# L0 cross-attention: keys normalised by features on GpSimd in four waiting steps, VectorE's norms in small pieces

## The chip, the cores and the metric

One Trainium2 chip, one core. The metric is the device time of one launch of a whole 12-layer kernel in microseconds; the kernel before took 3076.74 us (median of three runs, 3074.42 to 3076.98). The change touches one of the layers, L0's cross-attention (`l0_xattn`), which lies at the start.

## The reference

The input x is 8 x 64 x 256 and the context `ctx_1024` is 8 x 1601 x 256, all float32. The layer takes the normalised x as latents and attends over the context and the latents themselves:

```python
xn = layernorm(x, ln_x_g, ln_x_b)            # the context, 1601 tokens a batch
ln = layernorm(latents, ln_l_g, ln_l_b)      # 64 tokens a batch
q = (ln @ Wq) ...                            # 16 heads of 64
kv = concatenate([xn @ Wkv, ln @ Wkv])       # 1665 keys
qn = rmsnorm(q, qn_g) * scale;  kn = rmsnorm(k, kn_g)
sim = where(mask, einsum('bhid,bhjd->bhij', qn, kn), max_neg)
out = einsum('bhij,bhjd->bhid', softmax(sim), v) @ Wout + bout
```

Here layernorm is over the 256 features of a token (eps 1e-5) and rmsnorm over the 64 of a head.

## The kernel before, in words

The layer runs 64 steps: for each of 8 batches (b) eight steps (p), each of which does one pair of heads. Five instruction streams are written out by hand, one for an engine, and wait for each other by semaphores; the order inside a stream is the order of the code.

The context of a batch is held in two forms. `keys_tok` (the code's `xn`) has tokens on the partitions, 13 tiles of 128 tokens, and is used by the mix (probabilities times tokens; the values' projection comes after the mix, on 64 rows). `keys_feat` (`xnT`) has features on the partitions, 2 x 1665 columns, and is used by the projection of keys. Both have two buffers, one for the batch under work and one for the next.

The batch after is prepared inside the steps of the batch before: SP loads its tokens behind step 1; VectorE takes statistics (`ctx_stats`, bn_stats and bn_aggr, 7 and 6 tiles, at the end of steps 1 and 2), ScalarE makes the reciprocal root by Ln and Exp (`ctx_rstd`), VectorE normalises in place (`ctx_norm`, 7 tiles at the end of step 2 and 6 at the end of step 3, each L1385), GpSimd applies gain and bias (`gains`, L1558 and L1560) and then builds the mask row (`mask_row`, L1569). In steps 5 and 6 TensorE transposes the finished tokens of the next batch into features (`turn_keys`, L1727, 26 transposes a batch, in groups of 4, 3, 4 and 2 for each half of the features), and ScalarE and VectorE copy them out of PSUM (`keys_turned`, L1616 and L1441).

One step s on TensorE, in order: projection of the keys of step s+1, first half (L1742); transposes of the probabilities of step s-1, groups 0 and 1 (L1783); second half of the projection; groups 2 and 3; the transposes of the mixed sums of s-2 (L1814); the first part of the mix of s-1 (L1805); means of squares for s+1 (L1749); more mix; the scores of s (L1766); values of s-2 (L1823); more mix, an exchange of maxima between halves (L1791), the rest of the mix.

The same step on VectorE: copy of the keys' first half out of PSUM (L1446, 833 columns); copy of transposed probabilities (L1479, L1480); copy of the second half (L1446); L1479 and L1480 again; the product of keys and their scale, in two halves (`keys_normed`, L1456, both inputs in SBUF); the clamp of the mean squares of s+1 (`key_clamp`, L1450); the masked scores with their maximum, one for each head of the pair (`score_max`, L1466); the copy of a result (L1497); the negated maximum, the "shift" (L1471); and the division of the mix of s-1 (`divide`: L1487, L1489, L1492).

ScalarE squares the keys, copies transposed probabilities (L1644), makes the reciprocal norms of the keys of s+1 (L1625, L1627), stores them to DRAM (L1632, the scale rows) and then takes the exponentials of s (L1638), which wait for the shift. SP broadcasts the scale rows from DRAM to 2 x 64 partitions (`spread_scale`, L1340), and its loads for the next batch follow behind those in its queue. The scores' waits (`scores`, L1766) are for the product of s and the clamp of s+1.

## Time and profile before

| what | value |
|---|---|
| median of three runs | 3076.74 us (3074.42 to 3076.98) |
| the profiled execution's own time | 3077.33 us |
| its span | 3075.0 us |
| TensorE busy (PE) | 2774.9 us, 90% |
| VectorE busy (DVE) | 1690.4 us, 55% |
| ScalarE busy (ACT) | 1118.8 us, 36% |
| GpSimd busy (POOL) | 517.1 us, 17% |
| mix matmuls of this layer, L1805 | 431.2 us in 1664 |
| key projections of this layer, L1742 | 383.0 us in 1024 |
| mean granted clock of TensorE | 0.953 of full speed |

PE stands for TensorE, PEld for its weight loads, DVE for VectorE, ACT for ScalarE and POOL for GpSimd; SPq, ACTq and the like are an engine's queue at the issue of a DMA. A row of the timeline gives the start in microseconds from the start of the span, the length (of all instructions merged into the row, from the first's start to the last's end), engine, line of the kernel, operation, what is written <- what is read, shapes and count, and in brackets how long the engine stood idle before it and what released it. The first 16 of 40 slices of the span (77 us each) are this layer, and TensorE's busy share there is nearly always nine tenths.

### The profile page before, as it was taken

How to read it: one execution, taken by the hardware profiler on the slowest of the kernel's cores; microseconds unless marked ns; L12 is line 12 of the kernel's file. 1: busy time of each engine (PE TensorE's matmuls, PEld its weight loads, DVE VectorE, ACT ScalarE, POOL GpSimd, SP SyncE). 2: the span in 40 equal slices, each digit the busy share in tenths (PEclk: the TensorE clock that was granted, in tenths of full speed). 3: DMA queues.
4: the chain of work that ended last, by engine and by line, in shares of the span. 5: the costliest groups of instructions: out<-in, count | busy, mean ns of one | idle time of the engine just before them, and what ended most of it. 6: DMA issues, size and time to landing. Idle time of an engine off the chain costs nothing. (4 is left out here: it accounts for less than half of the span.)

```text
span 3075.0 us, 43440 instructions
## 1 busy us (share of the span) xinstructions
PE 2774.9 (90%) x17334; PEld 1876.2 (61%) x17334; DVE 1690.4 (55%) x3756; ACT 1118.8 (36%) x1993; POOL 517.1 (17%) x288
## 2 busy tenths in 40 slices
PE   5899999999999999789999977999996788979978
PEld 2566656566666666455565544665794456958846
DVE  5557575756566554545555545775452151057755
ACT  2343333333333332214555445662231161311123
POOL 2012020202020100000000000773001041045502
PEclk9899999999999999889999989999998997989989
DMA  4222232131322221131000000113686726743201
GB/s 149 49 54 71 52 77 71 46 82 46 77 51 72 46 57 35 58 133 44 23 33 33 1 6 15 46 42 107 239 309 193 227 56 245 276 161 141 70 13 35
DMA packets 93074, 272.45 MB, mean 89 GB/s; under 512 B 7874, under 2 KB 58074, under 8 KB 86218
## 3 DMA queue, kind: packets, MB, share of 16 engines
q1 hardware_dynamic: 88874, 260.70, 27.1%
q0 software_dynamic: 2976, 8.13, 0.7%
q8 instruction: 138, 2.26, 0.3%
q10 hardware_dynamic: 1024, 0.86, 0.1%
q14 instruction: 62, 0.51, 0.1%
HBM read 257.69 MB, written 11.45 MB: 88 GB/s over the span
## 5 line engine op out<-in xcount | busy, mean ns | idle before, releaser
L1805 PE MATMUL L_xattn_bank<-L_xattn_keys_tok,L_xattn_probsT 128*128 128x257 f32 x1664 | 431.2, 398 | 9.0 <-ACT L_xattn_probsT L1644 0.4
L1742 PE MATMUL L_xattn_wide<-L_xattn_keys_feat,weights_a 128*128 128x512 f32 (+2 forms) x1024 | 383.0, 517 | 1.3 <-DVE L_xattn_k_rnorm L1450 0.7
L1805 PEld LDWEIGHTS L_xattn_bank<-L_xattn_keys_tok,L_xattn_probsT 128*128 128x128 f32 x1664 | 300.3, 192 | 95.4 <-issue 34.4
L1742 PEld LDWEIGHTS L_xattn_wide<-L_xattn_keys_feat,weights_a 128*128 128x128 f32 x1024 | 190.8, 191 | 152.0 <-issue 125.3
L1446 DVE COPY L_xattn_k_normed<-L_xattn_wide 128x833 f32<-128x833 f32 (+1 forms) x128 | 131.0, 1024 | 183.2 <-PE L_xattn_wide L1742 183.2
L2751 DVE TENSOR_TENSOR_SCAN L_attn_state<-L_attn_decay,L_attn_banks 128x1024 f32<-128x1024 f32 x80 | 182.7, 2286 | 69.3 <-PE L_attn_banks L2953 61.3
L2021 DVE CUSTOM_DVE_ANT_0 L_xattn_scores<-L_xattn_banks,L_xattn_mask 128x512 f32<-128x512 f32 (+1 forms) x256 | 131.5, 570 | 151.8 <-issue 151.8
L1638 ACT ACTIVATE L_xattn_scores<-L_xattn_scores,L_xattn_neg_max 128x897 f32<-128x897 f32 x128 | 126.5, 1036 | 211.0 <-DVE L_xattn_neg_max L1471 211.0
L1558 POOL TENSOR_TENSOR L_xattn_keys_tok<-L_xattn_keys_tok,weights_a 128x1792 f32<-128x1792 f32 (+2 forms) x24 | 56.5, 2354 | 860.9 <-DVE L_xattn_keys_tok L1385 860.9
L2857 POOL TENSOR_TENSOR L_attn_state<-L_attn_state,L_attn_C_rows 128x1024 f32<-128x1024 f32 x80 | 188.7, 2360 | 70.0 <-DVE L_attn_state L2751 69.9
L1466 DVE CUSTOM_DVE_ANT_0 L_xattn_scores<-L_xattn_wide,L_xattn_mask_row 128x897 f32<-128x897 f32 x128 | 134.9, 1088 | 115.7 <-issue 115.7
L2953 PEld LDWEIGHTS L_attn_banks<-L_attn_B_diagonal,L_attn_dt_u_tok 128*128 128x128 f32 x1280 | 150.1, 193 | 66.3 <-issue 64.7
L2087 ACT ACTIVATE L_xattn_probsT<-L_xattn_banks 128x512 f32<-128x512 f32 (+1 forms) x208 | 122.7, 597 | 163.4 <-PE L_xattn_banks L2159 163.4
L3546 PE MATMUL L_ffn_banks<-L_ffn_slot_features,L_ffn_expert_w 128*128 128x128 f32 x1440 | 168.2, 277 | 3.0 <-DVE x_tok L3376 3.0
L2953 PE MATMUL L_attn_banks<-L_attn_B_diagonal,L_attn_dt_u_tok 128*128 128x128 f32 x1280 | 164.9, 283 | 3.9 <-ACT L_attn_B_diagonal L2813 3.9
L3546 PEld LDWEIGHTS L_ffn_banks<-L_ffn_slot_features,L_ffn_expert_w 128*128 128x128 f32 x1440 | 165.4, 194 | 3.9 <-DVE x_tok L3376 3.8
L1644 ACT ACTIVATE L_xattn_probsT<-L_xattn_bank 128x512 f32<-128x512 f32 x128 | 76.3, 596 | 230.4 <-PE L_xattn_bank L1783 230.4
L2159 PE MATMUL L_xattn_banks<-const,L_xattn_scores 128*128 128x128 f32 (+1 forms) x832 | 134.1, 288 | 24.7 <-DVE L_xattn_V L2012 10.7
L1783 PE MATMUL L_xattn_bank<-const,L_xattn_scores 128*128 128x128 f32 x896 | 120.8, 274 | 21.7 <-DVE L_xattn_probsT L1480 19.9
L1621 ACT ACTIVATE L_xattn_k_square<-L_xattn_k_normed 128x833 f32<-128x833 f32 (+1 forms) x128 | 115.2, 900 | 64.2 <-DVE L_xattn_k_normed L1446 61.1
L2159 PEld LDWEIGHTS L_xattn_banks<-const,L_xattn_scores 128*128 128x128 f32 (+1 forms) x832 | 88.8, 142 | 79.3 <-issue 45.8
L2844 POOL TENSOR_TENSOR L_attn_D_diagonal<-const,weights_a 128x256 f32<-128x256 f32 x2 | 1.2, 614 | 805.8 <-POOLq L909 805.8
(509 smaller groups left out, 4734.6 us busy)
## 6 DMA issues: line engine op xcount, KB each, us to landing
L_xattn_k_scale<-L_xattn_k_scale_rows SPq DMA_DIRECT2D x128, 417.0 KB, 5.0
L_xattn_ctx_feat<-in_ctx_feat SPq DMA_DIRECT2D x24, 1601.0 KB, 10.9
L_ffn_expert_w<-in_x_L_ffn SPq DMA_DIRECT2D x16, 2056.0 KB, 8.3
L_ffn_expert_w<-in_x_L_ffn SPq DMA_DIRECT2D x17, 1024.0 KB, 5.4
L_ffn_expert_w<-in_x_L_ffn SPq DMA_DIRECT2D x15, 1028.0 KB, 5.5
L_xattn_keys_tok<-in_ctx_tok SPq DMA_DIRECT2D x8, 1536.0 KB
L_attn_C_rows<-L_attn_c_rows SPq DMA_DIRECT2D x48, 256.0 KB, 3.2
L_xattn_ctx_tok<-in_ctx_tok SPq DMA_DIRECT2D x8, 1536.0 KB
```

The costliest lines, as they stand in the source:

```text
L1446: nc.vector.tensor_copy(kn[:, s % 2, a:a + n], ps).then_inc(k_copied, 1)
L1466: nc.vector.tensor_tensor_reduce(sc2[:, h, 0:SCORES], ps, mrow[b % 2][:, 1 - h:1 - h + SCORES], 1.0, -3.0e38, ALU.add, ALU.max, mx[:, h:h ...
L1638: nc.scalar.activation(sc2[:, h, 0:SCORES], sc2[:, h, 0:SCORES], ACT.Exp, bias=nm[:, h:h + 1]).then_inc(exp_ready, 1)
L1742: last = nc.tensor.matmul(wide[:, 2 * h + c, 0:n], wk[:, k, p * P:(p + 1) * P], xnT[b % 2][:, k, a:a + n], start=(k == 0), stop=(k == KT - 1))
L1805: last = nc.tensor.matmul(bS[:, 0:D + 1], pT[:, c, a, :, :].rearrange("p h q -> p (h q)"), xn[b % 2][:, t, :], start=(i == 0), stop=(i == ...
L2021: nc.vector.tensor_tensor_reduce(sc[:, j, a:a + n], ps[:, j, 0:n], mk[:, a:a + n], 1.0, -3.0e38, ALU.add, ALU.max, mx[:, j, c:c + 1]).then ...
L2087: nc.scalar.activation(pT[0:r, i % RING, :, :], ps[0:r, 6 + n % 2, :].rearrange("p (a n) -> p a n", n=P), ACT.Copy).then_inc(pT_ready, 1)
L2159: last = nc.tensor.transpose(ps[0:r, 6 + n % 2, j * P:(j + 1) * P], sc[:, j, t * P:t * P + r], L.ident)
L2751: nc.vector.tensor_tensor_scan(h[:, p % RING, :, :].rearrange("p m n -> p (m n)"), dA[:, p % RING, :, :].rearrange("p m n -> p (m n)"), ba ...
L2857: nc.gpsimd.tensor_tensor(state, state, C[:, g % C_RING, :].unsqueeze(1) .broadcast_to([P, 2, N]), ALU.mult).then_inc(hC_ready, 1)
L2953: last = nc.tensor.matmul(banks[:, i + j, t * P:(t + 1) * P], duT[d][:, t, m * P:(m + 1) * P], diag[:, g % DIAG_RING, t, :], start=True, s ...
L3546: last = nc.tensor.matmul(bank[:, c, :], w1[:, k, f:f + P], xT[:, j % 2, k, :], start=(k == 0), stop=(k == KT - 1))
```

## The change

For all batches but the first, `keys_feat` is no longer made by transposes. SP loads the context a second time, laid out by features (`load_feat`, behind step 2). VectorE's statistics and norms are cut into pieces of one to four tiles and stand at four places of a step (`between`: in front of the first copy of keys, in front of the second, behind the clamp, in front of the division). After the reciprocal roots, TensorE transposes the 26 columns of means and roots once (`turn_norms`, step 3's last group of transposes, which runs in the fifth step), VectorE copies the 26 x 128 result out, SP stores it to DRAM and broadcasts it to all partitions as two rows of 1601 columns (`spread_norms`, queued behind the scale rows of step 4). GpSimd then subtracts the mean and multiplies by the root over 128 x 1602, twice each (`keys_by_feature`), and ScalarE applies gain and bias, a column each, in one activation for each half of the features (`keys_gained`, step 6), and copies the 64 own keys (`own_keys`). The gains of the token form move to steps 6 and 7. In front of its subtractions, multiplications and the two gains GpSimd waits for VectorE's product of steps 4, 5, 6 and 7 (`keys_scaled`). The first batch is prepared as before. The weights grow by two columns each for gain and bias. (`-` and `+` lines of the diff follow, cut to its core: new semaphores and buffers, memsets of unused columns and unchanged names are left out.)

```diff
+                def load_feat(b):
+                    if b >= 2:
+                        sp.wait_ge(k_projected, 2 * NQ * (b - 1))
+                    feat = L.aps["ctx_feat"][b].rearrange("(k p) n -> p k n", p=P)
+                    sp.dma_start(xnT[b % 2][:, :, 0:FIRST], feat[:, :, 0:FIRST]).then_inc(feat_loaded[b % 2], 16)
+                    sp.dma_start(xnT[b % 2][:, :, SCORES:CTX + 1], feat[:, :, FIRST:CTX]).then_inc(feat_loaded[b % 2], 16)
+                def spread_norms(b):
+                    sp.wait_ge(norm_cols_ready, b)
+                    for i in range(2):
+                        sp.dma_start(norm_rows[b % 2, i].rearrange("(t n) -> t n", n=P), norm_cols[i:2 * TILES:2, :]
+                                     ).then_inc(norm_stored, 16)
+                    sp.wait_ge(norm_stored, 32 * b)
+                    if b >= 2:
+                        sp.wait_ge(feat_scaled, 2 * (b - 1))
+                    for i in range(2):
+                        sp.dma_start(norm_bc[:, i, 0:FIRST], norm_rows[b % 2, i:i + 1, 0:FIRST].broadcast_to([P, FIRST])
+                                     ).then_inc(norm_moved, 16)
+                        sp.dma_start(norm_bc[:, i, SCORES:CTX + 1],
+                                     norm_rows[b % 2, i:i + 1, FIRST:CTX].broadcast_to([P, CTX - FIRST])
+                                     ).then_inc(norm_moved, 16)
...
+                    if p == 2 and b < B - 1:
+                        load_feat(b + 1)
+                    if p == 4 and b < B - 1:
+                        spread_norms(b + 1)
...
                 def weights_turned(s, g):
                     h, a, n = GROUPS[g]
+                    b, p = divmod(s, NQ)
+                    if g == 3 and p == 3 and b + 1 < B:
+                        norms_turned(b + 1)
...
+                def norms_turned(b):
+                    dve.wait_ge(norm_turned, b)
+                    if b >= 2:
+                        dve.wait_ge(norm_stored, 32 * (b - 1))
+                    nc.vector.tensor_copy(norm_cols[:, :], bT[0:2 * TILES, 1, 384:384 + P]).then_inc(norm_cols_ready, 1)
+                stats_at = {(1, 2): range(0, 3), (1, 3): range(3, 7), (2, 0): range(7, 10), (2, 1): range(10, TILES)}
+                norm_at = {(2, 2): (range(0, 4),), (2, 3): (range(4, 6),), (3, 0): (range(6, 7), range(7, 9)),
+                           (3, 1): (range(9, 11),), (3, 2): (range(11, TILES),)}
+                def between(s, place):
+                    b, p = divmod(s, NQ)
+                    if b + 1 < B:
+                        if (p, place) in stats_at:
+                            ctx_stats(b + 1, stats_at[p, place])
+                        for tiles in norm_at.get((p, place), ()):
+                            ctx_norm(b + 1, tiles)
...
+                    between(s, 0)
                     if ahead:
                         key_copy(s + 1, 0)
                     if behind:
                         weights_turned(s - 1, 1)
+                    between(s, 1)
                     if ahead:
                         key_copy(s + 1, 1)
...
                     if ahead:
                         key_clamp(s + 1)
-                    if turns:
-                        keys_turned(b + 1, p - 5, 0)
+                    between(s, 2)
                     if s < STEPS:
                         score_max(s)
...
-                    if turns:
-                        keys_turned(b + 1, p - 5, 1)
-                    if s < STEPS and b + 1 < B:
-                        if p == 1:
-                            ctx_stats(b + 1, 0)
-                        if p == 2:
-                            ctx_stats(b + 1, 1)
-                            ctx_norm(b + 1, 0)
-                        if p == 3:
-                            ctx_norm(b + 1, 1)
+                    between(s, 3)
                     if behind:
                         divide(s - 1)
...
+                def keys_scaled(b, step):
+                    pool.wait_ge(kn_ready, 2 * (NQ * (b - 1) + step) + 2)
+
+                def keys_by_feature(b):
+                    pool.wait_ge(feat_loaded[b % 2], 32 * ((b + 1) // 2))
+                    pool.wait_ge(norm_moved, 64 * b)
+                    keys_scaled(b, 4)
+                    for k in range(KT):
+                        x = xnT[b % 2][:, k, 0:CTX + 1]
+                        nc.gpsimd.tensor_tensor(x, x, norm_bc[:, 0, :], ALU.subtract).then_inc(feat_shifted, 1)
+                    keys_scaled(b, 5)
+                    for k in range(KT):
+                        x = xnT[b % 2][:, k, 0:CTX + 1]
+                        pool.wait_ge(feat_shifted, 2 * (b - 1) + k + 1)
+                        nc.gpsimd.tensor_tensor(x, x, norm_bc[:, 1, :], ALU.mult).then_inc(feat_scaled, 1)
                 for b in range(B):
+                    if b:
+                        keys_by_feature(b)
+                        keys_scaled(b, 6)
                     gains(b, 0)
+                    if b:
+                        keys_scaled(b, 7)
                     gains(b, 1)
                     mask_row(b)
...
+                def keys_gained(b, k):
+                    act.wait_ge(feat_scaled, 2 * (b - 1) + k + 1)
+                    x = xnT[b % 2][:, k, 0:CTX + 1]
+                    g, o = at["ln_x_gc"] + k, at["ln_x_bc"] + k
+                    nc.scalar.activation(x, x, ACT.Identity, scale=w[:, g:g + 1], bias=w[:, o:o + 1]
+                                         ).then_inc(feat_ready, 1)
+                def own_keys(b):
+                    own = L.zT[:, :, b * S:(b + 1) * S]
+                    act.wait_ge(feat_ready, 3 * b - 1)
+                    nc.scalar.activation(xnT[b % 2][:, :, CTX + 1:KC], own[:, :, 0:S - 1], ACT.Copy)
+                    nc.scalar.activation(xnT[b % 2][:, :, FIRST:SCORES], own[:, :, S - 1:S], ACT.Copy).then_inc(feat_ready, 1)
...
-                    if b + 1 < B and p in (2, 3):
-                        ctx_rstd(b + 1, p - 2)
-                    if turns:
-                        keys_turned(b + 1, p - 5, 0)
-                        keys_turned(b + 1, p - 5, 1)
+                    if b + 1 < B and p == 2:
+                        ctx_rstd(b + 1, 1)
+                    if b + 1 < B and p == 6:
+                        for k in range(KT):
+                            keys_gained(b + 1, k)
+                        own_keys(b + 1)
                     if s < STEPS:
                         exponentials(s)
...
-                    if g < 2 and p in (5, 6) and b + 1 < B:
-                        pe.wait_ge((xT_act, xT_dve)[g], 4 * (b + 1) + 2 * (p - 5) + 2)
...
+                    if g == 3 and p == 3 and b + 1 < B:
+                        turn_norms(b + 1)
+
+                def turn_norms(b):
+                    pe.wait_ge(ctx_rstd_ready, 4 * b + 4)
+                    nc.tensor.transpose(bT[0:2 * TILES, 1, 384:384 + P], mv[:, :, :].rearrange("p t i -> p (t i)"),
+                                        L.ident).then_inc(norm_turned, 1)
...
-                    if turns:
-                        turn_keys(b + 1, p - 5, 0)
-                        turn_keys(b + 1, p - 5, 1)
```

## Rows read from the trace of the kernel before

**Rows 1.** The timeline of VectorE, the shift (L1471) of seven of the 64 steps.

```profile
97.77 0.16 DVE L1471 SCALAR_TENSOR_TENSOR L_xattn_neg_max<-L_xattn_max,L_xattn_bank 128x2 f32<-128x2 f32 x1 [0.48 <-PE L_xattn_bank L1791]
...
543.26 0.16 DVE L1471 SCALAR_TENSOR_TENSOR L_xattn_neg_max<-L_xattn_max,L_xattn_bank 128x2 f32<-128x2 f32 x1 [0.58 <-PE L_xattn_bank L1791]
...
560.15 0.16 DVE L1471 SCALAR_TENSOR_TENSOR L_xattn_neg_max<-L_xattn_max,L_xattn_bank 128x2 f32<-128x2 f32 x1 [0.57 <-PE L_xattn_bank L1791]
...
581.73 0.16 DVE L1471 SCALAR_TENSOR_TENSOR L_xattn_neg_max<-L_xattn_max,L_xattn_bank 128x2 f32<-128x2 f32 x1 [0.58 <-PE L_xattn_bank L1791]
...
598.86 0.16 DVE L1471 SCALAR_TENSOR_TENSOR L_xattn_neg_max<-L_xattn_max,L_xattn_bank 128x2 f32<-128x2 f32 x1 [0.60 <-PE L_xattn_bank L1791]
...
617.08 0.16 DVE L1471 SCALAR_TENSOR_TENSOR L_xattn_neg_max<-L_xattn_max,L_xattn_bank 128x2 f32<-128x2 f32 x1 [1.19 <-PE L_xattn_bank L1791]
...
1096.17 0.16 DVE L1471 SCALAR_TENSOR_TENSOR L_xattn_neg_max<-L_xattn_max,L_xattn_bank 128x2 f32<-128x2 f32 x1 [0.54 <-PE L_xattn_bank L1791]
```

**Rows 2.** The timeline of TensorE in the slow third step.

```profile
570.73 0.55 PE L1783 MATMUL L_xattn_bank<-const,L_xattn_scores 128*128 128x128 f32 x3 [2.85 <-DVE L_xattn_probsT L1480]
```

**Rows 3.** Stretches of time: busy us and count per engine, clock, DMA share, GB/s.

```profile
561.00:578.00 17.00, 14.02 (x61) 7.63 (x63) 14.06 (x31) 5.58 (x9) 7.43 (x2) 0.90 0.14 31
```

**Rows 4.** The timeline of VectorE from the second to the fourth step.

```profile
543.33 2.38 DVE L1370 BATCH_NORM_STATS2 L_xattn_ctx_stats<-L_xattn_keys_tok 128x6 f32<-128x256 f32 x7
...
562.93 2.35 DVE L1385 TENSOR_SCALAR L_xattn_keys_tok<-L_xattn_keys_tok,L_xattn_ctx_mean_var,L_xattn_ctx_rstd 128x256 f32<-128x256 f32 x7
...
565.90 3.32 DVE L1492 TENSOR_SCALAR L_xattn_mixed_tokens<-L_xattn_mixed_sum,L_xattn_rsum 128x256 f32<-128x256 f32 x1
...
584.45 2.23 DVE L1492 TENSOR_SCALAR L_xattn_mixed_tokens<-L_xattn_mixed_sum,L_xattn_rsum 128x256 f32<-128x256 f32 x1
...
590.87 2.69 DVE L1456 TENSOR_TENSOR L_xattn_k_normed<-L_xattn_k_scale,L_xattn_k_normed 128x834 f32<-128x834 f32 x2
...
596.01 1.09 DVE L1466 CUSTOM_DVE_ANT_0 L_xattn_scores<-L_xattn_wide,L_xattn_mask_row 128x897 f32<-128x897 f32 x1 [1.94 <-issue]
```

**Rows 5.** The timeline of GpSimd.

```profile
55.13 2.63 POOL L1558 TENSOR_TENSOR L_xattn_keys_tok<-L_xattn_keys_tok,weights_a 128x1280 f32<-128x1280 f32 x1 [1.52 <-DVE L_xattn_keys_tok L1385]
...
565.36 3.71 POOL L1558 TENSOR_TENSOR L_xattn_keys_tok<-L_xattn_keys_tok,weights_a 128x1792 f32<-128x1792 f32 x1 [111.52 <-DVE L_xattn_keys_tok L1385]
...
590.82 5.87 POOL L1569 TENSOR_SCALAR L_xattn_mask_row<-L_xattn_mask_bytes 64x896 f32<-64x896 uint8 x2
```

**Rows 6.** Groups of GpSimd instructions by shape: busy us, mean ns of one.

```profile
L721 POOL TENSOR_TENSOR L_ffn_experts_total<-L_ffn_experts_total,L_ffn_expert_out 128x1024 f32<-128x1024 f32 x7 | 16.5, 2353 | 24.5 <-ACT L_ffn_expert_out L765 24.4
```

**Rows 7.** The timeline of VectorE in a quiet step.

```profile
513.13 1.03 DVE L1446 COPY L_xattn_k_normed<-L_xattn_wide 128x833 f32<-128x833 f32 x1 [1.65 <-PE L_xattn_wide L1742]
...
518.50 1.97 DVE L1456 TENSOR_TENSOR L_xattn_k_normed<-L_xattn_k_scale,L_xattn_k_normed 128x834 f32<-128x834 f32 x2
...
528.13 0.35 DVE L1492 TENSOR_SCALAR L_xattn_mixed_tokens<-L_xattn_mixed_sum,L_xattn_rsum 128x256 f32<-128x256 f32 x1
```

**Rows 8.** The timeline of VectorE under GpSimd's operation at 55.13.

```profile
57.02 0.74 DVE L1415 SCALAR_TENSOR_TENSOR L_xattn_qT<-L_xattn_wide,L_xattn_q_gain,L_xattn_scores 128x512 f32<-128x512 f32 x1
```

**Rows 9.** The timeline of TensorE in the quiet step.

```profile
521.62 1.73 PE L1766 MATMUL L_xattn_wide<-L_xattn_k_normed,L_xattn_qT 64*64 64x512 f32 x16
```

**Rows 10.** The timeline of ScalarE and its queue in a quiet step.

```profile
505.59 1.00 ACTq L1632 DMA_DIRECT2D L_xattn_k_scale_rows<-L_xattn_k_rnorm  x2
509.55 1.98 ACT L1638 ACTIVATE L_xattn_scores<-L_xattn_scores,L_xattn_neg_max 128x897 f32<-128x897 f32 x2 [3.99 <-DVE L_xattn_neg_max L1471]
```

**Rows 11.** The timeline of SP's queue in the same step.

```profile
507.76 1.08 SPq L1340 DMA_DIRECT2D L_xattn_k_scale<-L_xattn_k_scale_rows  x2
```

**Rows 12.** DMA issues on the page: count, KB each, median us to landing.

```profile
L_xattn_k_scale<-L_xattn_k_scale_rows SPq DMA_DIRECT2D x128, 417.0 KB, 5.0
```

**Rows 13.** Stretches of 2 us: with the scale rows, and with the tokens.

```profile
510.00:512.00 2.00, 2.00 (x7) 1.01 (x6) 1.00 (x3) 1.53 (x2) 0.00 (x0) 1.00 1.04 240
...
530.00:532.00 2.00, 2.00 (x12) 1.28 (x11) 1.54 (x3) 1.41 (x2) 0.00 (x0) 1.00 1.09 343
```

More of the change, by code:

```diff
@@ L1363, in _, with ctx_stats @@
                 chain = Chain(dve, dve_chain)
-                def ctx_stats(b, piece):
-                    if piece == 0:
+                def ctx_stats(b, tiles):
+                    if tiles[0] == 0:
                         dve.wait_ge(ctx_loaded[b % 2], 32 * (b // 2) + 32)
-                    for t in range(*CTX_PIECES[piece]):
+                        if b >= 2:
+                            dve.wait_ge(norm_turned, b - 1)
+                    for t in tiles:
                         r = rows(t)
@@ L1372, in ctx_stats, with ctx_norm @@
                     take_wait(L, 3)
[L1373 removed]
+                    for t in tiles:
                         r = rows(t)
                         last = nc.vector.bn_aggr(mv[0:r, t, :], st[0:r, t, :])
[L1376 to L1380 removed]
+                    for a, c in CTX_PIECES:
+                        if tiles[-1] == c - 1:
+                            chain(last)
+                            nc.vector.tensor_scalar(ve[:, a:c], ve[:, a:c], EPS, None, ALU.add).then_inc(ctx_var_ready, 1)
+                def ctx_norm(b, tiles):
+                    piece = tiles[-1] // HALF_T
                     dve.wait_ge(ctx_rstd_ready, 4 * b + 2 * piece + 2)
[L1382 removed]
+                    for t in tiles:
                         r = rows(t)
@@ L1385, in ctx_norm @@
                         last = nc.vector.tensor_scalar(x, x, mv[0:r, t, 0:1], ve[0:r, t:t + 1], ALU.subtract, ALU.mult)
-                    last.then_inc(ctx_normed, 1)
+                    if tiles[-1] == CTX_PIECES[piece][1] - 1:
+                        last.then_inc(ctx_normed, 1)
                 norm_vector(L, dve, chain, ln_stats_ready, rstd_ready, z_ready)
```

54 lines of the change are left out of this document (31 added, 23 removed).

## The prediction

> **What bounds the kernel now.** I read the page first: its busy shares and slices, in the table above, show TensorE nearly always busy in this layer. Then I took the timeline of VectorE for the start of every step, one slow step on TensorE, VectorE and GpSimd, a quiet one, and last the DMAs. The layer under change runs 64 steps (8 batches of 8 pairs of heads), and each has one VectorE instruction, the shift (L1471), whose starts measure the steps [rows 1]. From the first shift at 97.77 to the first of the last batch at 1096.17, 56 steps take 998.4 us. A quiet step takes 16.89 us (543.26 to 560.15): TensorE is its bound. 56 quiet steps would take 945.8 us, so 52.6 us is all that this change can win. In the batch shown, the step from the third shift to the fourth (560.15 to 581.73) takes 21.58 instead of 16.89 (+4.69), the next 17.13 (+0.24), and the one with transposed keys 18.22 (+1.33); a second such step follows it.
>
> **Where +4.69 comes from.** TensorE stood 2.85 us before the last three transposes of the weights, for VectorE's copy L1480 [rows 2]. The granted clock of that stretch is 0.90 on average, where the two quiet stretches have 1.00 [rows 3, 13]: it fell behind the idle time, so the rest, some 1.8 us, is mostly matmuls at the lower level of 1.2 GHz. VectorE was late because six statistics, seven norms (2.35 us) and the last product of the division (L1492) stand together behind the shift [rows 4]. L1492 takes 0.35 us in a quiet step [rows 7] and 3.32 here: it waits for GpSimd's tensor_tensor of 565.36 to 569.07 [rows 5], as the norms have just released that. GpSimd can thus hold an operation of VectorE for its whole length.
>
> **What the change removes.** (1) The bunch on VectorE. (2) 26 transposes on TensorE, two steps of +1.33 each, and their copies on VectorE and ScalarE. (3) The +0.24: there the product of keys and scale (L1456) took 2.69 instead of 1.97, beside GpSimd's mask row from 590.82 [rows 4, 5, 7]. It was 0.72 late and the step 0.24: the product has 0.48 us of slack, which I need below. Of the 52.6 us, I leave 0.2 per batch to small excesses that no part touches (the first step of a batch), so 51.0 us are removable. Seven times the shown batch's 7.59 (4.69 + 0.24 + 2 x 1.33) would be 53.1, more than the whole excess; so I go by the total.
>
> **What it adds, on each engine.** I count from the first copy of keys in a quiet step (513.13 is 0). Then the product runs from +5.37 to +7.34, TensorE's scores, which wait for it and for the clamp behind it, start at +8.49, L1492 runs from +15.00 to +15.35, and the next copy is due at +16.9 [rows 7, 9].
>
> *VectorE.* Statistics cost 0.34 us a tile (2.38 for 7), with aggregation and chain some 1.5 us for three and 2.0 for four; a norm costs 0.34 [rows 4]. Behind the shift of the second step come four tiles, 2.0 us, of which about 0.9 lies beside the wait for the mix; then three more, 1.5, before the next copy of keys, where 1.6 us are free (+15.35 to +16.9). So that copy is some 0.9 late. Before the second copy there is about 2 us of waiting, into which the last three tiles (1.7) must fit, so about 0.5 remains at the product, the size of its slack. All other pieces are one to four norms, 0.3 to 1.4 us, in gaps of 1.6 to 2.1 such as the 1.94 before L1466 [rows 4]; only between shift and division is the gap smaller (about 0.9), with two norms of 0.7. Cost 0 to 0.3 a batch; if the cover went, the whole piece of 1.5.
>
> *TensorE.* One transpose of the norms a batch, 0.13 us by the transposes of [rows 2] (0.55 for 3 with a tail, so 0.1 to 0.2): 0.9 us for seven batches. It waits for the norms' Exp of two steps earlier, which is long done. The wait for ready keys moves to ScalarE's work a step earlier.
>
> *ScalarE.* Two activations over 1602 columns, by 1.98 us for two of 897 1.77 each, and two small copies, about 0.45 together: 4.0 us before the exponentials. There 3.99 us are idle, of which the two DMA issues take 1.00 [rows 10]: the exponentials start 1.0 us late. TensorE wants their first half, over at 510.6 in a quiet step, only behind the next projection of keys, whose copy L1446 starts at 513.13: 1.0 late is covered. Cost 0; bounds 0 to 0.5 a batch.
>
> *SP.* After VectorE's copy of the norms (about 0.3 us, at +4.6 in the fifth step, which moves the product inside its slack), SP issues two stores and waits until they have landed. The same sort of store took 2.17 us from ScalarE's issue at 505.59 to SP's next issue at 507.76 [rows 10, 11]. So SP issues the four broadcasts at about +7.2 to +9.2; the next scale rows are ready for SP at 507.76, which is 11.5 behind the copy of keys that comes 16.9 before 513.13: SP delays nobody. They queue behind the table in the DMA engines, though, and have until +22.3, the next product. The loads of features (1.6 MB) go out a step after those of tokens, each in a step of its own.
>
> *When is the table of norms there?* 128 partitions of 2 x 1601 floats are 1.64 MB. The scale rows (twice 64 partitions, 0.85 MB) move at 240 GB/s, the tokens (128 partitions) at 343 [rows 13]. Two scale DMAs, issued within 1.08 us, land 5.0 after their issue, so the second some 5.5 after the first issue [rows 11, 12]; 3.6 of it is data, 1.9 is latency. So the table is there at 7.2 + 1.9 + 4.8 = +13.9 at the high rate and 7.2 + 1.9 + 6.8 = +15.9 (+16.4 with gaps in the traffic) at the low one. I take +14.3, near the tokens' row, since all 128 partitions are written.
>
> The Trainium skill ("SBUF — State Buffer", the section on how DMA bandwidth depends on the ports that the partitions reach) says that a transfer to partitions 0 to 63 reaches half the ports, about 218 GB/s at most, and only one over 128 reaches them all. The two rows agree with that (240 and 343); by it the table comes at the early time, and by the scale rows' rate at the late one.
>
> *GpSimd.* Full-width operands cost 2.353 us for 1024 columns, so 3.68 for 1602; by the broadcast gains (3.71 for 1792) it would be 3.32 [rows 5, 6]. Two subtractions take 7.45 with their gap. From +14.3 they run until +21.75; the next product is due at 16.9 + 5.37 = +22.3. So they miss the product. The first one does hold L1492 (due +15.0) until +18.0, so the next copy of keys is 1.5 us late. In the fourth step of the batch shown L1492 took 2.23 us under GpSimd and the step still lost only its 0.24 [rows 1, 4]: this is covered. The two multiplications start behind the product (+7.4) and end at +14.9, just before L1492. The gains start likewise a step and two steps later (3.71 + 3.71, then 2.63 twice and 0.73 twice), the mask row behind them (5.87) ends at about +20.2 and reaches into L1492's time, which has 1.6 us of room. What is queued behind GpSimd's new waits is wanted later: the mask row by the next batch's first L1466 at about +27, the gained tokens a step after that. The score maxima (L1466: one input in PSUM) lie under these: L1466 kept its 1.09 us beside the mask row, and L1415, with an input in PSUM too, ran within 0.74 us wholly under a GpSimd tensor_tensor from 55.13 to 57.76 [rows 4, 5, 8]. Cost 0 to 0.3.
>
> **Sum.** 51.0 - 0.9 (transposes) - 7 x 0.3 (what VectorE's pieces and the table leave) = 48.0. The profiled execution took 3077.33 us (span 3075.0), which makes 3029.3; the median of the runs lies 0.6 lower: 3029.
>
> **Rivals.**
> *The table comes late* (21%). At +16.4 the second subtraction ends at +23.9, the product waits 1.6, less 0.48: 1.1 us a batch, 7.8 us: 3037. At +18 it would be 2.7, 19 us, 3048. For it: the broadcast rows' own rate. Against: they go to half the partitions.
> *The pieces don't fit* (9%). Statistics in the second and third step push the product by another 1.5 us or more, or a wait for the square roots' Exp holds VectorE: 10 to 30 us less gain, 3040 to 3060. For it: two adjacent pieces of 3.5 us. Against: seven tiles stood behind the shift before and that step still took 16.89.
> *Slower: both subtractions before both halves of the product* (4%). If the table lands at about +21, each half waits for one of them: 7.4 - 0.5 = 6.9, and the clock falls as in [rows 3], about 1.6 more: 8.5 x 7 = 59.5 against the 50.1 won, 3087. It decides from some 8 us a batch, and needs a table at 130 GB/s.
> *It doesn't act* (2%): the gain is spent wholly on such waits, 3077.
> *Forecast* (64%): 3023 to 3035.
>
> About 0.2% (6 us) is what a measurement can tell here. Faster 0.95, within 0.02, slower 0.03 (the slower rival's milder forms fall inside 6 us). Range 3022 to 3047: it holds the forecast and most of the late table.
>
> **What would show it.** The shifts of the third and fourth step 16.9 apart; no transposes of keys after the first batch; GpSimd's first subtraction at +14 to +15 and L1456 at 1.97 us in the sixth step; PEclk 1.00 throughout. Wrong if L1456 of that step takes over 2.6 us, if any product waits for its scale rows, or if L1466 grows beyond 1.1 us under a GpSimd operation.

## The result, and the profile after

The changed kernel takes 3035.49 us (median of 4 runs, 3033.59 to 3043.81) against 3075.58 for the kernel before on the same chip (3072.79 to 3076.98): ratio 0.9869, 95% interval 0.9853 to 0.9885. The profiled execution took 3034.73 us. The forecast was 3029, its range 3022 to 3047. The first row is the span by core, the other the busy time by engine.

```profile
core 0: 3032.9 us, clock 0.955
...
PE 2745.7 (91%) x17159; PEld 1849.0 (61%) x17159; DVE 1654.0 (55%) x3739; ACT 1128.3 (37%) x1993; POOL 609.0 (20%) x316
```

The steps keep the prediction's names: the "third step" is the stretch from the third shift of a batch to the fourth; every other step (second, fifth to eighth) is named by the shift that ends it.

The timeline of VectorE, to be read beside [rows 1] and [rows 4]; line numbers are those of the changed kernel (the shift is L1515 now, the product L1500, the last product of the division L1545):

```profile
97.01 0.16 DVE L1515 SCALAR_TENSOR_TENSOR L_xattn_neg_max<-L_xattn_max,L_xattn_bank 128x2 f32<-128x2 f32 x1 [0.68 <-PE L_xattn_bank L1887]
...
310.45 2.97 DVE L1500 TENSOR_TENSOR L_xattn_k_normed<-L_xattn_k_scale,L_xattn_k_normed 128x834 f32<-128x834 f32 x2
...
539.90 0.16 DVE L1515 SCALAR_TENSOR_TENSOR L_xattn_neg_max<-L_xattn_max,L_xattn_bank 128x2 f32<-128x2 f32 x1 [0.58 <-PE L_xattn_bank L1887]
...
556.79 0.16 DVE L1515 SCALAR_TENSOR_TENSOR L_xattn_neg_max<-L_xattn_max,L_xattn_bank 128x2 f32<-128x2 f32 x1 [0.58 <-PE L_xattn_bank L1887]
...
560.56 1.03 DVE L1490 COPY L_xattn_k_normed<-L_xattn_wide 128x833 f32<-128x833 f32 x1 [1.65 <-PE L_xattn_wide L1833]
...
575.46 3.25 DVE L1545 TENSOR_SCALAR L_xattn_mixed_tokens<-L_xattn_mixed_sum,L_xattn_rsum 128x256 f32<-128x256 f32 x1
...
582.83 1.97 DVE L1500 TENSOR_TENSOR L_xattn_k_normed<-L_xattn_k_scale,L_xattn_k_normed 128x834 f32<-128x834 f32 x2
...
590.59 0.16 DVE L1515 SCALAR_TENSOR_TENSOR L_xattn_neg_max<-L_xattn_max,L_xattn_bank 128x2 f32<-128x2 f32 x1 [0.58 <-PE L_xattn_bank L1887]
...
607.48 0.16 DVE L1515 SCALAR_TENSOR_TENSOR L_xattn_neg_max<-L_xattn_max,L_xattn_bank 128x2 f32<-128x2 f32 x1 [0.58 <-PE L_xattn_bank L1887]
...
624.83 0.16 DVE L1515 SCALAR_TENSOR_TENSOR L_xattn_neg_max<-L_xattn_max,L_xattn_bank 128x2 f32<-128x2 f32 x1 [0.58 <-PE L_xattn_bank L1887]
...
1049.46 0.16 DVE L1515 SCALAR_TENSOR_TENSOR L_xattn_neg_max<-L_xattn_max,L_xattn_bank 128x2 f32<-128x2 f32 x1 [0.54 <-PE L_xattn_bank L1887]
```

The third step (539.90 to 556.79) takes 16.9 where it took 21.58, and the sixth and seventh (the second of them from 590.59 to 607.48) 16.9 where two took 18.2. The eighth is longer in every batch, here 17.35 (607.48 to 624.83) instead of 16.9, and so is the second from the second batch on, some 17.07 instead of 16.9. The sixth took 17.09, 17.41 and 16.98 in the first three batches. The 56 steps take 952.45 us against 998.4: 45.95 less, where 48.0 was forecast. The next two fences are the timelines of GpSimd and of SP's queue.

```profile
304.47 7.13 POOL L1636 TENSOR_TENSOR L_xattn_keys_feat<-L_xattn_keys_feat,L_xattn_norm_rows 128x1602 f32<-128x1602 f32 x2 [80.83 <-DMA L_xattn_norm_rows<-L_xattn_norm_table]
...
574.97 7.18 POOL L1636 TENSOR_TENSOR L_xattn_keys_feat<-L_xattn_keys_feat,L_xattn_norm_rows 128x1602 f32<-128x1602 f32 x2 [78.97 <-DMA L_xattn_norm_rows<-L_xattn_norm_table]
584.88 6.00 POOL L1641 TENSOR_TENSOR L_xattn_keys_feat<-L_xattn_keys_feat,L_xattn_norm_rows 128x1602 f32<-128x1602 f32 x2 [2.72 <-DVE L_xattn_k_normed L1500]
601.77 3.72 POOL L1614 TENSOR_TENSOR L_xattn_keys_tok<-L_xattn_keys_tok,weights_a 128x1792 f32<-128x1792 f32 x1 [10.90 <-DVE L_xattn_k_normed L1500]
605.58 3.73 POOL L1616 TENSOR_TENSOR L_xattn_keys_tok<-L_xattn_keys_tok,weights_a 128x1792 f32<-128x1792 f32 x1
```

```profile
565.36 1.58 SPq L1342 DMA_DIRECT2D L_xattn_norm_table<-L_xattn_norm_cols  x2
568.06 0.34 SPq L1348 DMA_DIRECT2D L_xattn_norm_rows<-L_xattn_norm_table  x1
...
574.95 1.14 SPq L1373 DMA_DIRECT2D L_xattn_k_scale<-L_xattn_k_scale_rows  x2
```

Counted from the fifth step's first copy of keys at 560.56, the stores go out at +4.8, the broadcasts at +7.5, the subtractions run from +14.4 to +21.6, and the product starts at +22.3 undisturbed (1.97 us). L1545, due at +15, takes 3.25 us instead of 0.35 under the subtractions, and the step still takes 16.9. In four of the seven batches the subtractions start only behind it, at +15.1 to +16.3.

Last, the timelines of TensorE and of ScalarE, at the start of the eighth step and in the second step of the next batch:

```profile
607.31 1.11 PE L1904 MATMUL L_xattn_bank<-L_xattn_keys_tok,L_xattn_probsT 128*128 128x257 f32 x4
608.60 3.06 PE L1833 MATMUL L_xattn_wide<-L_xattn_keys_feat,weights_a 128*128 128x512 f32 x8 [0.18 <-ACT L_xattn_keys_feat L1741]
...
650.45 1.98 PE L1904 MATMUL L_xattn_bank<-L_xattn_keys_tok,L_xattn_probsT 128*128 128x257 f32 x8 [0.34 <-ACT L_xattn_probsT L1721]
```

```profile
604.78 3.34 ACT L1734 ACTIVATE L_xattn_keys_feat<-L_xattn_keys_feat,weights_a 128x1602 f32<-128x1602 f32 x2 [1.10 <-issue]
608.14 0.31 ACT L1740 ACTIVATE L_xattn_keys_feat<-z_feat 128x126 f32<-128x126 f32 x1
608.36 0.19 ACT L1741 ACTIVATE L_xattn_keys_feat<-z_feat 128x2 f32<-128x2 f32 x1
608.46 1.96 ACT L1715 ACTIVATE L_xattn_scores<-L_xattn_scores,L_xattn_neg_max 128x897 f32<-128x897 f32 x2
```

TensorE would go on right behind its mix (over at 608.4), but the first projection of the next batch's keys waits for ScalarE's last small copy of 608.36. That is the eighth step's excess of 0.44 us. The idle time in the row is only 0.18, since the rows of matmuls overlap where nothing waits: without the wait (part 5) this projection starts 0.95 us behind the start of the mix row instead of 1.29, and takes 2.96 instead of 3.06.

### The profile page after: what moved, and what is told of

It reads as the page before. It is cut to its first block and busy times, and to the rows that moved or that the text cites. A ratio compares the mean times of both kernels' runs of the same rounds, so it can differ in the third digit from the quotient of the medians.

```text
span 3032.9 us, 43162 instructions
## 1 busy us (share of the span) xinstructions
PE 2745.7 (91%) x17159; PEld 1849.0 (61%) x17159; DVE 1654.0 (55%) x3739; ACT 1128.3 (37%) x1993; POOL 609.0 (20%) x316
## 5 line engine op out<-in xcount | busy, mean ns | idle before, releaser
L1510 DVE CUSTOM_DVE_ANT_0 L_xattn_scores<-L_xattn_wide,L_xattn_mask_row 128x897 f32<-128x897 f32 x128 | 134.9, 1088 | 96.7 <-issue 96.7
L1636 POOL TENSOR_TENSOR L_xattn_keys_feat<-L_xattn_keys_feat,L_xattn_norm_rows 128x1602 f32<-128x1602 f32 x14 | 50.1, 3598 | 578.8 <-DMA L_xattn_norm_rows<-L_xattn_norm_table 578.8
L2187 ACT ACTIVATE L_xattn_scores<-L_xattn_scores,L_xattn_neg_max 128x1601 f32<-128x1601 f32 x64 | 103.5, 1618 | 80.6 <-DVE L_xattn_neg_max L2116 80.6
L1500 DVE TENSOR_TENSOR L_xattn_k_normed<-L_xattn_k_scale,L_xattn_k_normed 128x834 f32<-128x834 f32 x128 | 128.1, 1043 | 5.0 <-DMA L_xattn_k_scale<-L_xattn_k_scale_rows 3.0
```

The costliest lines, as they stand in the source:

```text
L1500: nc.vector.tensor_tensor(k, spread[:, 2 * x:2 * x + 2, :], k, ALU.mult).then_inc(kn_ready, 1)
L1510: nc.vector.tensor_tensor_reduce(sc2[:, h, 0:SCORES], ps, mrow[b % 2][:, 1 - h:1 - h + SCORES], 1.0, -3.0e38, ALU.add, ALU.max, mx[:, h:h ...
```

## The experiments

"The layer" below is the 56 steps from the first shift to that of the last batch, in one profiled execution.

**1. The old kernel with GpSimd's waits alone** (e1):

```diff
 for b in range(B):
+    if b: pool.wait_ge(kn_ready, 2 * (NQ * (b - 1) + 3) + 2)
     gains(b, 0)
+    if b: pool.wait_ge(kn_ready, 2 * (NQ * (b - 1) + 4) + 2)
     gains(b, 1)
```

> The kernel before, where alone GpSimd's two gains wait for VectorE's product of keys and scale of the fourth and the fifth step (transposes of keys and the bunched statistics and norms stay). Theory H (the slow third step comes from GpSimd holding VectorE's last product of the division, 3.32 instead of 0.35 us, and the bunch alone fits into the slack): the third step falls from 21.58 to about 16.9 to 17.5, 4.1 to 4.7 us a batch, some 28 to 31 us in all: 3045 to 3049. Rival B (the bunch of six statistics and seven norms is itself too long; the pieces are what won): the third step stays above 19.5 and the kernel gains less than 14 us: 3062 or more.

Measured: 3044.73 us (3040.56 to 3045.22), ratio 0.9874 (0.9852 to 0.9896); the layer 966.7, 31.7 less. The timeline of VectorE, second to fourth shift of a batch, and L1492 (the old numbering) behind the third; then that of GpSimd:

```profile
528.48 0.16 DVE L1471 SCALAR_TENSOR_TENSOR L_xattn_neg_max<-L_xattn_max,L_xattn_bank 128x2 f32<-128x2 f32 x1 [0.57 <-PE L_xattn_bank L1795]
...
545.38 0.16 DVE L1471 SCALAR_TENSOR_TENSOR L_xattn_neg_max<-L_xattn_max,L_xattn_bank 128x2 f32<-128x2 f32 x1 [0.58 <-PE L_xattn_bank L1795]
...
551.13 0.35 DVE L1492 TENSOR_SCALAR L_xattn_mixed_tokens<-L_xattn_mixed_sum,L_xattn_rsum 128x256 f32<-128x256 f32 x1
...
562.38 0.16 DVE L1471 SCALAR_TENSOR_TENSOR L_xattn_neg_max<-L_xattn_max,L_xattn_bank 128x2 f32<-128x2 f32 x1 [0.58 <-PE L_xattn_bank L1795]
```

```profile
556.71 3.73 POOL L1558 TENSOR_TENSOR L_xattn_keys_tok<-L_xattn_keys_tok,weights_a 128x1792 f32<-128x1792 f32 x1 [108.40 <-DVE L_xattn_k_normed L1456]
```

The bunch of norms is still there, and L1492 starts late behind it, but it takes 0.35 us instead of 3.32 [rows 4], and the step is 17.0 instead of 21.58. The bunch alone costs 0.1; the slow step was made by GpSimd's hold at the end of the bunch. Two thirds of the layer's gain are these two waits: 30.0 of the 31.7 us in the slow steps, and 1.7 in the steps behind them (17.13 before, 16.9 now), where the mask row no longer lies beside the product. The times of the whole don't show this share: e1's ratio of 0.9874 and the change's 0.9869 have intervals that overlap.

**2. The change with the bunch back** (e2):

```diff
-stats_at = {(1, 2): range(0, 3), (1, 3): range(3, 7), (2, 0): range(7, 10), ...}
-norm_at = {(2, 2): (range(0, 4),), (2, 3): (range(4, 6),), ...}
+stats_at = {(1, 3): range(0, HALF_T), (2, 3): range(HALF_T, TILES)}
+norm_at = {(2, 3): (range(0, HALF_T),), (3, 3): (range(HALF_T, TILES),)}
```

and ScalarE's second reciprocal root a step later.

> The changed kernel with VectorE's statistics and norms in bunches as before (7 tiles, then 6 and 7, then 6, in front of the division), and ScalarE's second root a step later. Theory H: GpSimd is silent in these steps, so the third step takes 16.9 to 17.4 and the kernel stays within 4 us of the changed one. Rival B: the third step takes 19 to 21 us, and the kernel loses 14 to 29 us.

Measured: 3041.4 us in one run; the layer 953.99 (+1.5), the step from the third shift to the fourth 16.99. So the small pieces are worth 0.1 us a batch, 0.7 in all; another 1.0 is in the sixth steps of the first four batches, whose products were late by up to 1.3 us in this run, less 0.2 in the very first stretch between shifts. Whether the bunch or the traffic of that execution made those products late stays open.

**3. The change without GpSimd's four waits** (e3): `keys_scaled` does nothing.

> The changed kernel without GpSimd's four waits for VectorE's product; it still waits for the table, the features and its own results. If the waits are what keeps GpSimd off VectorE: the multiplications follow the subtractions at once, hold the product of the sixth step (1.97 us) to 4 to 7 us, and the gains behind them hold further operations of VectorE; steps five to eight grow by 2 to 9 us a batch, 3050 to 3100. Rival (the waits don't act, GpSimd would be clear of VectorE anyway): within 3 us of the changed kernel.

Measured: 3081.36 us in one run; the layer 994.69, 42.2 more than with the waits, nearly the whole gain. VectorE and GpSimd in the sixth step of the fourth batch:

```profile
598.60 6.89 DVE L1500 TENSOR_TENSOR L_xattn_k_normed<-L_xattn_k_scale,L_xattn_k_normed 128x834 f32<-128x834 f32 x2
```

```profile
590.67 7.20 POOL L1636 TENSOR_TENSOR L_xattn_keys_feat<-L_xattn_keys_feat,L_xattn_norm_rows 128x1602 f32<-128x1602 f32 x2 [103.04 <-DMA L_xattn_norm_rows<-L_xattn_norm_table]
597.84 6.78 POOL L1641 TENSOR_TENSOR L_xattn_keys_feat<-L_xattn_keys_feat,L_xattn_norm_rows 128x1602 f32<-128x1602 f32 x2
604.58 4.50 POOL L1614 TENSOR_TENSOR L_xattn_keys_tok<-L_xattn_keys_tok,weights_a 128x1792 f32<-128x1792 f32 x1
```

The two engines take turns: each half of the product (1 us by itself) waits for a multiplication, and the gains, 3.7 us with the waits, take 4.50 here, as they wait for a half of the product. The sixth step takes up to 24.4 us. This is the mechanism of the slower rival, here with the multiplications in the place of the subtractions, brought about by leaving the waits out.

**4. The table of norms in halves of 64 partitions** (e4), so that it lands late:

```diff
-sp.dma_start(norm_bc[:, i, 0:FIRST], norm_rows[b % 2, i:i + 1, 0:FIRST].broadcast_to([P, FIRST])
+for r in (slice(0, S), slice(S, P)):
+    sp.dma_start(norm_bc[r, i, 0:FIRST], norm_rows[b % 2, i:i + 1, 0:FIRST].broadcast_to([S, FIRST])
```

and the same for the other part.

> The changed kernel with each of the four broadcasts of the norm table cut into two over 64 partitions, eight DMAs in all. By the rate of the scale rows (240 GB/s or less, and eight issues) the table lands 2 to 3.5 us later, at +16.2 to +17.7 of the fifth step, GpSimd's second subtraction ends at +23.4 to +24.9, and the product of the sixth step, due at +22.3, takes 3.1 to 4.6 us instead of 1.97; with 0.48 us of slack 0.6 to 2.1 us a batch, 4 to 15 us. Rival (only bytes count, or the threshold lies elsewhere): the subtraction starts where it did, no step grows.

Measured: 3056.98 us in one run; the layer 975.96, 23.5 more. Product, subtractions and scores in one sixth step, and a stretch of 2 us while the table moved (columns as in [rows 13]):

```profile
593.84 5.03 DVE L1501 TENSOR_TENSOR L_xattn_k_normed<-L_xattn_k_scale,L_xattn_k_normed 128x834 f32<-128x834 f32 x2
```

```profile
589.93 7.12 POOL L1637 TENSOR_TENSOR L_xattn_keys_feat<-L_xattn_keys_feat,L_xattn_norm_rows 128x1602 f32<-128x1602 f32 x2 [82.91 <-DMA L_xattn_norm_rows<-L_xattn_norm_table]
```

```profile
599.52 2.44 PE L1858 MATMUL L_xattn_wide<-L_xattn_k_normed,L_xattn_qT 64*64 64x512 f32 x16 [2.50 <-DVE L_xattn_k_rnorm L1495]
```

```profile
582.00:584.00 2.00, 2.00 (x16) 1.71 (x12) 2.00 (x6) 0.00 (x0) 0.00 (x0) 1.00 0.97 236
```

The subtractions started at +17.5 to +19.2 instead of +14.4 to +16.3, later than expected, and ended at +24.6 to +27.1. Several things changed at once: from 582 to 590 the DMA engines were busy nearly all the time at 217 to 238 GB/s, where the table in one piece moved at 356 and 362; the last of the eight broadcasts went out at +12.2 to +13.0 instead of the last of four at +8.8 to +9.3; and the step's scale rows, issued at +13.4, came among them. No run parts these, but engines that are never idle point to the rate. The product was then up to 3.7 us late, 3.1 in the rows; TensorE stood 2.50 before the scores, and the 16 matmuls of these took 2.44 instead of 1.73 [rows 9]: the granted clock averaged 0.90 from 589 to 606, at 1.2 GHz for a while behind the idle time. In the last batch, where the product was 2.2 late and the clock stayed up, the step cost 1.68: 2.2 less the slack of 0.48. The rival of the late table is thus real, and 3.0 us of landing (the mean of seven batches) cost 3.4 us a batch.

**5. The two terms that the prediction missed** (e5, e6):

```diff
-if b + 1 < B and p == 6:
-    for k in range(KT):
-        keys_gained(b + 1, k)
+if b + 1 < B and p == 5:
+    keys_gained(b + 1, 0)
+if b + 1 < B and p == 6:
+    keys_gained(b + 1, 1)
     own_keys(b + 1)
```

e6 also takes TensorE's waits for the normed tokens and the latents from the front of a batch's first mix, ahead of the keys that precede it.

> The changed kernel with ScalarE's first activation for the next batch's keys (keys_gained of half 0) a step earlier, in front of the exponentials of step 5, and the second one and the own keys in step 6 as they are. Theory: the eighth step's 17.33 us is TensorE waiting for ScalarE's four operations in one row; with 1.67 us of them moved it falls to 16.9, 3.0 us in all, and no other step grows: the first multiplication is over at about +27.3, the exponentials there wait for the shift until about +30. Rival (the wait is for the own keys or the shift, not for the row's length): 17.33 stays. Second rival (the exponentials of step 5 come late instead): another step grows by 0.4.

> As the one before, and TensorE's two waits for the gained tokens and the latents stand before the second half of the projection of keys instead of in the row of four waits in front of the first mix of a batch. Theory: the second step of a batch falls from 17.07 to 16.9 (the extra waits are worked off while TensorE is busy), 1.2 us; with the other edit 4.2 us for the layer, 3031 if the layers behind take what they took. Rival (the tokens themselves are late): the second step stays or grows.

Measured: e5 3030.38 us in one run, the layer 949.61 (2.8 less), every eighth step 16.9. Its second batch has a sixth step of 17.74; the product there was 1.3 us late behind a table that came at +16.6, so it isn't the second rival's late exponentials. e6 3033.61 us (3030.65 to 3039.47), ratio 0.9857 (0.9832 to 0.9881), the layer 948.06 (4.4 less), second step 16.9 too. TensorE in e5 at the start of the eighth step, and in e6 at the first mix of the batch:

```profile
605.66 1.11 PE L1905 MATMUL L_xattn_bank<-L_xattn_keys_tok,L_xattn_probsT 128*128 128x257 f32 x4
606.61 2.96 PE L1834 MATMUL L_xattn_wide<-L_xattn_keys_feat,weights_a 128*128 128x512 f32 x8
```

```profile
647.37 2.01 PE L1902 MATMUL L_xattn_bank<-L_xattn_keys_tok,L_xattn_probsT 128*128 128x257 f32 x8
```

The 0.18 is gone, and the 0.34 is back to the 0.14 of a quiet step, which is too short for the row to name.

**6. The rows of the table swapped** (e7): the means, which the subtractions read, in the second row of the tile and the other norms in the first.

```diff
-sp.dma_start(norm_rows[b % 2, i].rearrange(...), norm_cols[i:2 * TILES:2, :]
+sp.dma_start(norm_rows[b % 2, 1 - i].rearrange(...), norm_cols[i:2 * TILES:2, :]
-... norm_bc[:, 0, :], ALU.subtract)
+... norm_bc[:, 1, :], ALU.subtract)
```

and `norm_bc[:, 0, :]` for the multiplications.

> The changed kernel with the two rows of the norm table in each other's place, so that GpSimd subtracts row 1 and multiplies by row 0. If the place of the operand makes a subtraction 3.59 us and a multiplication 3.02, the lengths change sides (3.0 and 3.6); if the operation does, they stay. The time of the kernel moves by less than 3 us either way.

```profile
440.13 6.00 POOL L1636 TENSOR_TENSOR L_xattn_keys_feat<-L_xattn_keys_feat,L_xattn_norm_rows 128x1602 f32<-128x1602 f32 x2 [80.72 <-DMA L_xattn_norm_rows<-L_xattn_norm_table]
448.28 7.13 POOL L1641 TENSOR_TENSOR L_xattn_keys_feat<-L_xattn_keys_feat,L_xattn_norm_rows 128x1602 f32<-128x1602 f32 x2 [2.15 <-DVE L_xattn_k_normed L1500]
```

Now the subtractions take 3.02 each and the multiplications 3.59; in the changed kernel it is the other way round (3.60 and 3.02). The length goes with the row of the operand, not with the operation. The two subtractions take 1.1 us less, so that with the table at +14.7 to +16.6 every sixth step takes 16.9: the layer 951.59, 0.9 less. One run took 3038.06 us.

**7. The changed kernel again** (e8).

> The changed kernel once more, to stand beside the second one on the same chip and to see how far the layers behind this one differ between runs: within 4 us of 3035, the steps of the layer as they were within 1 us in sum, the table of norms landing at +14.4 to +16.3.

Measured: 3035.32 us (3032.21 to 3039.1), ratio 0.9857 (0.9833 to 0.9882); the layer 952.40.

**8. The kernel before again, and with the change's memory alone** (e9, e10): behind the last shift of the layer all programs are the same, but the profiled executions are not equally long there.

> The kernel before, unchanged, profiled a second time. Behind the last shift of the layer the profiled execution of before took 1865.9 us, and those of the seven kernels that carry the change 1869.4 to 1875.3; that part of the program is the same in all. Theory R: this spread is from run to run, then this profile lies anywhere between 1866 and 1875 as likely as the others. Theory T: the changed kernels pay some 4 to 5 us there for a reason of their own, then this one lies at 1864 to 1867 again, and so does the whole at 3074 to 3078 us. The layer itself: 56 steps in 998.4 +/- 0.5 us by both.

```diff
+norm_cols = sb("norm_cols", [2 * TILES, P])
+norm_rows = nc.dram_tensor(name + "norm_table", (2, 2, TILES * P), F32, kind="Internal").ap()
+norm_bc = sb("norm_rows", [P, 2, CTX + 1])
```

> The kernel before with only the change's memory added and never used: the table in HBM, the two tiles norm_cols and norm_rows in SBUF, and two columns more in the tile of weights. Theory A (the places of the tiles and tensors in memory that follow set the 4 to 5 us behind the layer): behind the last shift 1869 to 1875 us and the whole 3079 to 3083. Theory R (run to run) and a theory C (the changed instructions themselves, their code or the state that they leave): like the kernel before, 1864 to 1867 by C, anywhere by R. The 56 steps take 998.4 +/- 0.5 in all.

Measured: 3077.21 us (ratio 0.9996, 0.9981 to 1.0010) and 3078.66 (1.0006, 0.9991 to 1.0022). Behind the last shift: 1867.9 and 1866.2 us. With the first profile and e1, the four kernels with the old layer take 1865.9 to 1867.9; the nine with the new one, the version of part 9 among them, 1869.4 to 1875.9. The ranges don't meet, so chance from run to run (theory R) is unlikely, and theory A falls by e10. What is left is C, the changed instructions or the state that they leave, and no run tells how.

The layer itself is not the same in each execution of the old kernel either: 995.47 us in e9, since three of its slow steps took 19.95 to 19.97 us; in the first profile one did. One of them in windows (columns as in [rows 3]), and TensorE in it:

```profile
558.00:575.00 17.00, 14.02 (x79) 8.07 (x78) 14.69 (x34) 6.10 (x11) 7.42 (x2) 1.00 0.14 32
```

```profile
567.82 0.55 PE L1783 MATMUL L_xattn_bank<-const,L_xattn_scores 128*128 128x128 f32 x3 [2.85 <-DVE L_xattn_probsT L1480]
```

TensorE stood the same 2.85 us as in [rows 2], but the granted clock stayed at 1.00 where [rows 3] have 0.90. So of the 4.69 us of such a step 1.63 (21.58 less 19.95) are the clock, and they don't come each time.

**9. All three improvements together** (e11: e6 and e7).

> The version with ScalarE's gains split and TensorE's waits moved, and the rows of the table swapped as well. The 56 steps: 948.06 us less the 0.8 that the late products of the sixth steps cost, so 947.2 to 947.6, with 16.9 us in every sixth step. The whole 3029 to 3035 us: 0.8 better than without the swap, which this measurement can't tell.

Measured: 3031.76 us (3029.93 to 3034.19), ratio 0.9842 (0.9824 to 0.9861); the layer 947.49, every sixth and eighth step 16.9. It has the shortest layer of all; its whole is 3.7 us below the median of the changed kernel, on another chip and with intervals that overlap. Behind the layer it took 1875.9 us, the most of all.

## Why the prediction was right, and where it was off

**The slow third step.** Right in size and cause: GpSimd's hold of L1492 and the clock behind TensorE's idle time. The prediction named the bunch and the hold together; e1 and e2 part them: 4.6 of the 4.69 us were the hold with what follows from it, 0.1 the bunch. The prediction's first item of what is removed, "the bunch on VectorE", is thus right only in that GpSimd no longer starts at its end. Its 1.8 us for the clock were 1.6.

**The steps with transposed keys, and the +0.24.** Right: 16.9 in all three, but for the sixth steps of the first three batches (see the slack).

**The table of norms.** Forecast at +14.3, range +13.9 to +16.4; it came at +14.4 to +16.3 over seven batches, the stores and the broadcasts within 0.8 us of their forecast times. The first row shows the rate in the fourth batch (+14.4), the others the latest table (+16.3, the second batch), for which GpSimd waited until 304.47 (columns as in [rows 13]):

```profile
572.00:574.00 2.00, 2.00 (x12) 1.74 (x11) 1.27 (x4) 0.12 (x1) 0.00 (x0) 1.00 0.98 356
...
300.00:302.00 2.00, 2.00 (x12) 1.74 (x11) 0.89 (x4) 0.49 (x1) 0.00 (x0) 1.00 0.96 362
...
302.50:304.00 1.50, 1.50 (x5) 0.76 (x4) 0.87 (x3) 0.98 (x2) 0.00 (x0) 1.00 0.07 26
```

That is the tokens' rate (343) and not the scale rows' (240), in both batches. So +16.3 lies where the prediction's low rate would put it, but the cause is another: nearly all of the table was there by +14.3, and for the last 1.5 us the share of busy DMA engines was 0.07, about one of sixteen. The first and third batch show the same (0.07 for over a microsecond). Why one engine ends late there stays open. The Trainium skill ("SBUF — State Buffer", on the ports that the partitions reach) says that only a transfer over all 128 partitions reaches all ports. The traces agree in direction: 356 GB/s here, 217 to 238 in e4 with halves of 64 partitions. The prediction also said that the two rows agree with the Trainium skill's 218 GB/s at most for 64 partitions; 240 is above it, so those two agree in direction only; a row counts everything that the core moved.

**The slack of 0.48.** Right. In the second batch the subtractions ended at +23.4, the product took 2.97 us (310.45) instead of 1.97, 1.0 late, and the step was 0.52 longer. In the first and third batch it was 0.7 and 0.6 late, for 0.2 and 0.1. Over seven batches the late table cost 0.8 us. So the rival of the late table came about in small. The first subtraction lay at +14 to +15, as forecast, in three batches of seven, and a sign that the prediction had named for being wrong was there: this product took over 2.6 us in two batches (2.65 and 2.97). Its other signs were not: L1510 (L1466 before) took at most 1.10 us in all its 128 instances, 42 of which started under an operation of GpSimd, no product of these steps waited for its scale rows, and the mean granted clock over the 56 steps was 1.00 (0.99 before).

**GpSimd under the division.** Right: L1545 took 3.25 to 3.50 us in three batches, and the step took 16.9. In the other four the table came too late to hold it.

**ScalarE.** Here a step failed. The prediction let the wait for ready keys move "to ScalarE's work a step earlier" and asked only what becomes late behind ScalarE's 4.0 us: the exponentials. They were covered, as it said. But the first projection of the eighth step waits for the 4.0 us themselves, which end at 608.55, just behind the end of the mix at 608.4: 0.44 us a batch, 3.1 in all. e5 removes it.

**TensorE.** The transposes of the norms were forecast at 0.9 us and cost nothing: they lie in idle time of 0.14 us that every such step has. The waits in front of a batch's first mix were not priced: the keys no longer take the wait for the normed tokens, so it stands there, with three others, and the idle time is 0.34 instead of 0.14: 0.17 in each of six batches, with 0.1 in the first batch 1.1 in all. e6 removes it. That it is the number of waits in a row that costs the time is argued and not shown: e6 moves two of them and shows only that they were it.

**VectorE's pieces.** With the table they were forecast at 2.1 us; all but the 0.8 of the table is within 0.1.

**The sum.** The excess over 56 quiet steps is 6.6 us instead of 4.6 (1.6 old, 3.1 for ScalarE, 1.1 for the waits, 0.8 for the table): 2.0 of the miss. The profiled execution is 5.4 above the forecast of 3029.3: these 2.0; 4.4 behind the layer; 0.2 in the last batch; less 0.8 ahead of the layer and 0.5 outside the span. The 4.4 is the term that the prediction did not have: it took what lies behind the layer as the same. The median of 3035.49 is in the range, but just above the 3023 to 3035 that the prediction gave 64%. The 998.4 that its sum starts from is itself one execution's: with e9's 995.47 the layer's gain is 43 us instead of 46.

**Behind the layer.** Part of it is the clock, at other places in each execution. TensorE at the output projection of this layer, in the changed kernel and then in the same kernel's second profile:

```profile
1175.33 0.66 PE L1922 MATMUL L_xattn_bank<-L_xattn_mixed_tokensT,weights_a 128*64 128x64 f32 x8 [0.47 <-ACT L_xattn_mixed_tokensT L1727]
1176.31 15.32 PE L1967 MATMUL L_xattn_wide<-weights_a,L_xattn_qT 128*128 128x256 f32 x64 [0.32 <-DVE L_xattn_qT L1550]
```

```profile
1176.55 0.46 PE L1922 MATMUL L_xattn_bank<-L_xattn_mixed_tokensT,weights_a 128*64 128x64 f32 x8 [0.47 <-ACT L_xattn_mixed_tokensT L1727]
1177.35 14.08 PE L1967 MATMUL L_xattn_wide<-weights_a,L_xattn_qT 128*128 128x256 f32 x64 [0.34 <-DVE L_xattn_qT L1550]
```

After nearly the same idle times the granted clock fell in the one (0.64 from 1176 to 1180) and not in the other (1.00): 1.2 us. Time at the lower clock behind the layer, worked out from the granted clock of stretches of 2 us, was 236 to 243 us in the old kernels and 236 to 253 in the new ones, so it explains the longest executions at most. It explains nothing of the 4.4 us between the first two profiles, which both have 243. The excess isn't spread evenly: one stretch, from the end of an attention layer into the feed-forward layer behind it, between the same two of ScalarE's instructions (2091.6 to 2210.8 in the kernel before, 2049.6 to 2171.7 in the changed one), took 119.2 to 120.0 us in the four old kernels and 120.5 to 122.5 in the nine new ones. That is 3.0 of the 4.4. Its cause stays open.

## What to carry to other kernels

An operation of GpSimd that becomes ready as VectorE ends a piece of work can hold VectorE's next operation for nearly its whole length, as it did here with L1492 and the product of keys, whose operands all lie in SBUF (the maxima, with an input in PSUM, kept their 1.09 us); a wait that puts it behind VectorE's last urgent one can cost nothing and here gave two thirds of the layer's gain. When work is moved to another engine, price not only what is queued behind it but the first consumer of its result. Here a layer shorter by 46 us in its profile made the whole shorter by 40 (medians) to 43 (profiled executions), so compare the stage itself in the trace where variants differ by a few us.

## What the runs showed of the hardware

- GpSimd's tensor_tensor over 128x1602 floats took 3.57 to 3.65 us with its second operand in the first row of a tile and 3.02 in the second, 6408 bytes further on in each partition, whatever the operation; swapped rows swapped the times. The prediction's 3.68 held for the first alone.
- The hold works both ways: a multiplication of 3.02 us took 3.80 when half a product of VectorE came in first.
- A table over 128 partitions moved at 356 and 362 GB/s; with twice as many DMAs of 64 partitions each the core moved 217 to 238, and it came about 3 us later.
- A transfer can end late with its rate unchanged: for 1.5 us behind 362 GB/s a share of only 0.07 of the DMA engines was busy, and GpSimd waited for it.
